# Attention loop of a perceiver block: key transposes and value products moved into the projections, with fewer value and probability buffers

## The chip, the core and the metric

The kernel runs on one core of a Trainium2 chip, as one program with five engines: TensorE (PE, with its weight loads listed as PEld), VectorE (DVE), ScalarE (ACT), GpSimd (POOL) and SyncE (SP, which issues the DMAs). The metric is the device time in microseconds. The kernel before was timed three times; its median is 3072.03 us (3068.97 to 3072.42).

## The reference

A perceiver block on 256 query tokens of width 512: a cross attention over a context of 25088 rows, a linear self attention, and an expert feed-forward part. Only the cross attention is touched. It has 16 heads of width 32 and a sigmoid in place of a softmax, so that nothing has to be normalised over the context:

```python
qh = (q @ Wq.T).reshape(B, Lq, H, D).transpose(0, 2, 1, 3)
kh = (k @ Wk.T).reshape(B, Lk, H, D).transpose(0, 2, 1, 3)
vh = (v @ Wv.T).reshape(B, Lk, H, D).transpose(0, 2, 1, 3)
qh = _layernorm(qh, gq, bq) * scale
kh = _layernorm(kh, gk, bk)
attn = jax.nn.sigmoid(jnp.einsum('bhqd,bhkd->bhqk', qh, kh))
x = jnp.einsum('bhqk,bhkd->bhqd', attn, vh)
```

## The kernel before

The context is cut into 196 tiles of 128 rows. One step of a loop handles one tile, four steps are written out per turn of the loop, and the steps are pipelined by hand: in step r TensorE projects tile r, turns and scores the keys of tile r-1, and adds up the values of tile r-2. Each engine has an instruction list of its own in a fixed order; semaphores that count upwards connect them. A wait for "tile r" is a wait for a count worked out by `n_of`.

The TensorE work of a step, in the words used below:

- P, `projection` (L1029): 24 matmuls of 512 columns with 128x128 weights. The first 12 make the centred keys in `kv_ps[:, 0]`, the last 12 make the values in `kv_ps[:, 1]`. Each operand is split in a high and a low part, hence three products for each of four pieces.
- T, `turn_keys` (L1050): four 128x128 transposes of the normalised keys `k_n` into `kv_ps[:, 1]`, the place of the values. So it waits until the values were copied away (`v_copied`), and the next value projection waits until the turned keys were split (`kt_lo_made`).
- S0 and S1, `scores` (L1063): for each half of the heads 24 matmuls with weights of 32 rows and 128 columns, four of them side by side in the array, so six groups of four. Each half fills the same four banks `s_ps`, so S1 of a tile waits for the sigmoid of S0 of that tile.
- A, `attend` (L1075): the products of probabilities and values, with weights of 128 rows and 32 columns, again four side by side. The profile lists 32 matmuls for both halves, eight groups of four.

The order of TensorE in a step is T(r-1), P(r) 1 to 24, S0(r-1), A(r-2) both halves, S1(r-1).

The others: ACT runs in a step the sigmoid of S1(r-2) (L496, 128x2048 elements), the square and a copy of the new keys (L502, L505), and the sigmoid of S0(r-1). DVE splits the turned keys (L676, L678), makes the high part of the next context tile (L669), sums the squares (L687), copies the values (L683) and scales the keys (L694). POOL makes the low part of the next context tile (L407), and for the keys an addition (L413) and a power of -0.5 (L417); the latter two stand behind the former in its list. SP loads context tiles three ahead.

There are four buffers `v_sb` for the values and three `probs` for the probabilities: S0's alternate between two, S1's always use the third.

Of the kernel before, what the change touches and what calls it, by code (L numbers as in the profile page):

```python
# [12 lines left out]
TOK, C, H, D = 256, 512, 16, 32  # L13
NK = 25088
P = 128
TT, CT = TOK // P, C // P
KT = NK // P
HG = P // D
# [77 lines left out]
def perceiver_block(nc, a, out, NKT=KT):  # L96
    f32, f32r = mybir.dt.float32, mybir.dt.float32r
    ALU, ACT, AX = mybir.AluOpType, mybir.ActivationFunctionType, mybir.AxisListType.X
    nq = (NKT - 4) // UNROLL
    life = ExitStack()  # L100
    with life:
        def sb(name, shape, dt=f32, scope=life):
            return scope.enter_context(nc.sbuf_tensor(name, shape, dt))
# [56 lines left out]
        attn = ExitStack()  # L160
# [14 lines left out]

        kt_hi = sb("kt_hi", [P, NG, P], f32r, attn)
        kt_lo = sb("kt_lo", [P, NG, P], f32r, attn)
        v_sb = [sb(f"v_sb{i}", [P, C], f32, attn) for i in range(4)]
        probs = [sb(f"probs{i}", [P, HG, 2, TOK], f32, attn) for i in range(3)]
        zeros = probs[-1][:, 0].rearrange("p j t -> p (j t)")  # L180
        psum_a = ExitStack()
        o_ps = ps("o_ps", [P, NG, TOK], psum_a)
        kv_ps = ps("kv_ps", [P, 2, C], psum_a)
        s_ps = ps("s_ps", [P, HG, 2, TOK], psum_a)
# [68 lines left out]
        s_made, probs_made, av_made = sem("s_made"), sem("probs_made"), sem("av_made")  # L253
        v_copied = sem("v_copied")
# [14 lines left out]
        def wait(eng, s, v):  # L269

            if not isinstance(v, int) or v > 0:
                eng.wait_ge(s, v)

        def n_of(it, r, per=1, more=0):

            if isinstance(it, int):
                return per * (4 * it + r) + more
            return it * (4 * per) + (per * r + more)

        def probs_of(r, half):  # L280

            return probs[2] if half else probs[r % 2]

        def is_first(it, r, t):

# [203 lines left out]
        def _(act):  # L489
            s = nc.scalar  # L490

            def sigmoid(it, r, half):

                act.wait_ge(s_made, n_of(it, r, 2, half + 1))
                wait(act, av_made, n_of(it, r, 2, 2 if half else -1))
                s.activation(probs_of(r, half)[:], s_ps[:], ACT.Sigmoid).then_inc(probs_made, 1)  # L496

            def square(it, r):

# [114 lines left out]
        def _(dve):  # L614
            v = nc.vector
# [55 lines left out]
            def split_turned(it, r):  # L671

                dve.wait_ge(t_made, n_of(it, r, 1, 1))
                wait(dve, s_made, n_of(it, r, 2))
                turned = kv_ps[:, 1].rearrange("p (g k) -> p g k", g=NG)
                v.tensor_copy(kt_hi[:], turned).then_inc(kt_hi_made, 1)  # L676
                dve.wait_ge(kt_hi_made, n_of(it, r, 1, 1))
                v.tensor_tensor(kt_lo[:], turned, kt_hi[:].bitcast(f32), ALU.subtract).then_inc(kt_lo_made, 1)  # L678

            def copy_values(it, r):  # L680
                dve.wait_ge(v_made, n_of(it, r, 1, 1))
                wait(dve, av_made, n_of(it, r, 2, -4))
                v.tensor_copy(v_sb[r % 4][:], kv_ps[:, 1]).then_inc(v_copied, 1)  # L683

            def sum_squares(it, r):
                dve.wait_ge(k_sq_made, n_of(it, r, 1, 1))
# [9 lines left out]

            def step(it, r, keys=True, more=True):

                split_turned(it, r - 1)
                if more:  # L700
                    high_part(it, r + 1)
                if keys:
                    sum_squares(it, r)
                    copy_values(it, r)
                    normalise(it, r)


# [12 lines left out]
            for c in range(CT):  # L720
# [25 lines left out]
            link(v.tensor_copy(q_hi[:], q_turned_in))  # L746
            v.tensor_tensor(q_lo[:], q_turned_in, q_hi[:].bitcast(f32), ALU.subtract)\
                .then_inc(once("q_parts_made"), 1)
            copy_values(0, 0)
            normalise(0, 0)  # L750


# [245 lines left out]
        def _(pe):  # L998
            t = nc.tensor
# [12 lines left out]
            for c in range(CT):  # L1012
                for b in range(CT):
                    dst = s_ps[:, c, b // 2, (b % 2) * P:(b % 2 + 1) * P]
                    ins = t.matmul(dst, wk[:, b, c * P:(c + 1) * P], centre[:], start=True, stop=True)
# [4 lines left out]
            for i in range(TT):  # L1020
                for c in range(CT):
                    ins = t.matmul(kv_ps[:, i], x_t[:, c, i * P:(i + 1) * P], wq[:, c],
                                   start=(c == 0), stop=(c == CT - 1))
# [10 lines left out]
            def projection(it, r, first, last):  # L1034

                for m in range(first, last):
                    if m == 0:
                        pe.wait_ge(ctx_lo_made, n_of(it, r, 1, 1))
                        wait(pe, k_kept, n_of(it, r))
                    if m == 12:  # L1040
                        wait(pe, v_copied, n_of(it, r))
                        wait(pe, kt_lo_made, n_of(it, r))
                    project(it, r, m // 12, m % 12 // 3, m % 3)

            def turn_keys(it, r):

                pe.wait_ge(k_normed, n_of(it, r, 1, 1))
                pe.wait_ge(v_copied, n_of(it, r, 1, 1))
                for grp in range(NG):
                    ins = t.transpose(kv_ps[:, 1, grp * P:(grp + 1) * P],  # L1050
                                      k_n[:, HG * grp:HG * grp + HG].rearrange("p h d -> p (h d)"), ident[:])
                ins.then_inc(t_made, 1)

            def scores(it, r, half):

                pe.wait_ge(kt_lo_made, n_of(it, r, 1, 1))
                wait(pe, probs_made, n_of(it, r, 2, half))
                for j in range(2):
                    grp = 2 * half + j
                    for n, (k, q) in enumerate(((kt_hi, q_hi), (kt_hi, q_lo), (kt_lo, q_hi))):  # L1060
                        for h in range(HG):
                            own = slice(D * h, D * h + D)
                            ins = t.matmul(s_ps[:, h, j], k[own, grp], q[own, grp],  # L1063
                                           start=(n == 0), stop=(n == 2))
                ins.then_inc(s_made, 1)

            def attend(it, r, half):

                pe.wait_ge(probs_made, n_of(it, r, 2, half + 1))
                pe.wait_ge(v_copied, n_of(it, r, 1, 1))  # L1070
                for j in range(2):
                    grp = 2 * half + j
                    for h in range(HG):
                        first = P * grp + D * h
                        ins = t.matmul(o_ps[D * h:D * h + D, grp], v_sb[r % 4][:, first:first + D],  # L1075
                                       probs_of(r, half)[:, h, j], start=False, stop=False, skip_group_check=True)
                ins.then_inc(av_made, 1)

            def step(it, r, project_it=True):

                turn_keys(it, r - 1)
                if project_it:
                    projection(it, r, 0, 24)
                scores(it, r - 1, 0)
                if not too_early(it, r - 2):
                    attend(it, r - 2, 0)
                    attend(it, r - 2, 1)
                scores(it, r - 1, 1)

            def too_early(it, r):  # L1090
# [6 lines left out]
            for i in range(2):  # L1097
                ins = t.matmul(o_ps[:, 2 * i:2 * i + 2].rearrange("p g t -> p (g t)"), zeros[:, 0:P],
                               zeros, start=True, stop=True)
# [6 lines left out]
            for grp in range(NG):  # L1106
                for i in range(TT):
                    ins = t.transpose(q_turned_in[:, grp, i * P:(i + 1) * P],
                                      big[1][:, i, grp * P:(grp + 1) * P], ident[:])
# [16 lines left out]
            for i in range(TT):  # L1126
                for c in range(CT):
                    ins = t.matmul(pm[:, i], o_t[:, c, i * P:(i + 1) * P], wp[:, c],
                                   start=(c == 0), stop=(c == CT - 1))
# [4 lines left out]
            for i in range(TT):  # L1134
                pe.wait_ge(once("x1_t_made"), i + 1)
                wait(pe, once("qkv_copied"), i)
                for k in range(3):
                    for c in range(CT):
                        ins = t.matmul(pm[:, k], mid_t[:, c, i * P:(i + 1) * P],  # L1139
                                       qkv_w[:, c, k * C:(k + 1) * C], start=(c == 0), stop=(c == CT - 1))  # L1140
                ins.then_inc(once("qkv_made"), 1)
            pe.sem_inc(w_used, 2)
            for i in range(TT):
                pe.wait_ge(once("qk_made"), i + 1)
                for k in range(2):
                    for grp in range(NG):
                        ins = t.transpose(po[:, 2 * i + k, grp * P:(grp + 1) * P],
                                          qk_max[:, i, k * C + grp * P:k * C + (grp + 1) * P], ident[:])
# [36 lines left out]
            for i in range(TT):  # L1185
                for c in range(CT):
                    ins = t.matmul(pm[:, 2 + i], mid_t[:, c, i * P:(i + 1) * P], out_w[:, c],  # L1187
                                   start=(c == 0), stop=(c == CT - 1))
# [5 lines left out]
            for i in range(TT):  # L1194
                for c in range(CT):
                    ins = t.matmul(m_ps[:, 0, i * E:(i + 1) * E], nx_t[:, c, i * P:(i + 1) * P],
                                   router_w[:, c], start=(c == 0), stop=(c == CT - 1))
            ins.then_inc(once("logits"), 1)
            pe.wait_ge(once("gates"), 1)
            for i in range(TT):  # L1200
                ins = t.transpose(m_ps[0:E, 1, i * P:(i + 1) * P], rt[:, 5, i], ident[:])
            ins.then_inc(once("gates_turned"), 1)
            pe.wait_ge(once("gate_split"), 1)
            for e in range(E):

                for part in range(2):
                    ins = t.matmul(f_ps[:, e // 2, (e % 2) * TOK:(e % 2 + 1) * TOK],
                                   pick[:, e:e + 1].to_broadcast([E, P]), gate_parts[:, part],
                                   start=(part == 0), stop=(part == 1))
# [137 lines left out]
```

## Time and profile before

| | |
|---|---|
| median of three runs | 3072.03 us |
| the profiled execution | 3068.97 us |
| its span, first to last instruction | 3067.2 us |
| the attention loop | from about 75 us to about 1985 us of the span |
| TensorE busy | 2923.6 us, 95% |
| VectorE, ScalarE, GpSimd busy | 49%, 46%, 37% |

Times of rows are microseconds from the start of the span. A timeline row has a start, a duration, engine, line, operation, written tile, read tiles, and a count of instructions merged; square brackets tell how long the engine had been idle and which engine released it. The matmuls overlap, so the distance between two starts tells their pace, and the duration is a latency. For four matmuls side by side one row stands for the group.

### The profile page before, as it was taken

Reading aid. Unit: us, or ns where it says so; the run is one execution under the profiler, and the core shown is the slowest. Engines: PE = TensorE matmul, PEld = TensorE weight load, DVE = VectorE, ACT = ScalarE, POOL = GpSimd, SP = SyncE. Lnnn points to the kernel's source line nnn. Section 1 sums busy time; section 2 is a strip of 40 time slices with the busy share of each in tenths; the row PEclk is TensorE's granted clock in tenths of the full one; section 3 lists DMA queues with packets and bytes.
Section 4 is the critical chain, followed back from the end, with each engine's and each line's share of the span. In section 5 each row is a group of like instructions: output and inputs, shape, how many; then the busy total and the mean of one; then the engine's idle time right before and its main releaser. Section 6 shows DMA issues by size and latency. Waiting matters only on the chain.

```text
span 3067.2 us, 71038 instructions
## 1 busy us (share of the span) xinstructions
PE 2923.6 (95%) x28530; PEld 2355.4 (77%) x28530; DVE 1505.4 (49%) x2020; ACT 1417.4 (46%) x1277; POOL 1137.0 (37%) x856
## 2 busy tenths in 40 slices
PE   6999999999999999999999999976999999999998
PEld 4777777777777777777777777745998988999987
DVE  5333333333333333333333333346477766578877
ACT  1444444445444444444444444422445445455444
POOL 3444444444444444444444444401031423032322
PEclk8999999999999999999999999987999999999999
DMA  5000000000000000000000001001545445555443
GB/s 199 28 24 27 27 27 24 27 27 24 27 27 26 26 27 27 24 27 27 24 27 27 27 24 27 11 28 69 192 166 184 173 165 192 192 179 179 157 162 141
DMA packets 53229, 231.78 MB, mean 76 GB/s; under 512 B 6040, under 2 KB 6296, under 8 KB 31776
## 3 DMA queue, kind: packets, MB, share of 16 engines
q1 hardware_dynamic: 53152, 230.73, 22.1%
q8 instruction: 50, 0.82, 0.1%
q14 instruction: 27, 0.22, 0.0%
HBM read 230.19 MB, written 0.52 MB: 75 GB/s over the span
## 4 chain that ended last, share of the span: by engine, by line
PE 75%; ACT 13%; DVE 6%; issue 4%; DMA 1%; POOL 1%; ACTq 0%; DVEq 0%; SPq 0%; POOLq 0%
PE kv_ps L1029 34%; PE f_ps L1270 18%; PE s_ps L1063 12%; ACT probs L496 12%; PE kv_ps L1050 4%; PE y_ps L1257 4%; DVE stage L884 1%; DMA w_raw<-w_dram 1%; ACT w_hi L535 1%; DVE w_lo L628 1%; PE pm L1139 1%; DVE h_hi L883 1%; DVE sums L921 1%; POOL h_lo L470 0%; PE pm L1187 0%
## 5 line engine op out<-in xcount | busy, mean ns | idle before, releaser
L496 ACT ACTIVATE probs<-s_ps 128x2048 f32<-128x2048 f32 x392 | 737.0, 1880 | 713.6 <-PE s_ps L1063 713.6
L407 POOL TENSOR_TENSOR ctx_lo<-ctx_raw,ctx_hi 128x512 fp32r<-128x512 f32 x196 | 252.0, 1286 | 905.3 <-DVE ctx_hi L669 905.3
L417 POOL TENSOR_TENSOR k_var<-k_var,neg_half 128x16 f32<-128x16 f32 x196 | 570.7, 2912 | 15.5 <-POOL k_var L413 0.2
L470 POOL TENSOR_TENSOR h_lo<-stage,h_hi 128x256 f32 x240 | 255.3, 1078 | 695.8 <-DVE h_hi L886 388.1
L628 DVE TENSOR_TENSOR w_lo<-w_raw,w_hi 128x2048 fp32r<-128x2048 f32 x164 | 383.1, 2340 | 168.4 <-ACT w_hi L535 167.6
L1270 PE MATMUL f_ps<-h_hi,w_hi 128*128 128x256 f32 x1536 | 428.0, 279 | 14.8 <-POOL h_lo L470 14.8
L1270 PE MATMUL f_ps<-h_lo,w_hi 128*128 128x256 f32 x1536 | 426.8, 278 | 0.0
L1270 PE MATMUL f_ps<-h_hi,w_lo 128*128 128x256 f32 x1536 | 426.6, 278 | 0.0
L1075 PE MATMUL o_ps<-probs,v_sb 128*32 128x256 f32 x6272 | 380.9, 383 | 1.0 <-ACT probs L496 1.0
L535 ACT ACTIVATE w_hi<-w_raw 128x2048 fp32r<-128x2048 f32 x164 | 313.1, 1912 | 138.7 <-DMA w_raw<-w_dram 100.9
L1029 PE MATMUL kv_ps<-wk_hi,ctx_hi 128*128 128x512 f32 x784 | 324.1, 413 | 1.5 <-issue 1.5
L676 DVE CAST kt_hi<-kv_ps 128x512 fp32r<-128x512 f32 x196 | 135.5, 691 | 373.5 <-PE kv_ps L1050 373.5
L1029 PE MATMUL kv_ps<-wk_lo,ctx_hi 128*128 128x512 f32 x784 | 307.9, 393 | 0.0
L1029 PE MATMUL kv_ps<-wk_hi,ctx_lo 128*128 128x512 f32 x784 | 307.7, 392 | 0.0
L1029 PE MATMUL kv_ps<-wv_hi,ctx_hi 128*128 128x512 f32 x784 | 305.1, 389 | 0.0
L1029 PE MATMUL kv_ps<-wv_hi,ctx_lo 128*128 128x512 f32 x784 | 305.0, 389 | 0.0
L1029 PE MATMUL kv_ps<-wv_lo,ctx_hi 128*128 128x512 f32 x784 | 304.8, 389 | 0.0
L1270 PEld LDWEIGHTS f_ps<-h_hi,w_hi 128*128 128x128 f32 x1536 | 291.1, 190 | 15.7 <-POOL h_lo L470 15.6
L1063 PEld LDWEIGHTS s_ps<-q_hi,kt_hi 32*128 32x128 f32 x3136 | 153.7, 183 | 192.4 <-ACT probs L496 117.6
L1063 PE MATMUL s_ps<-q_hi,kt_hi 32*128 32x256 f32 x3136 | 269.6, 329 | 29.2 <-ACT probs L496 11.5
L1270 PEld LDWEIGHTS f_ps<-h_hi,w_lo 128*128 128x128 f32 x1536 | 291.2, 190 | 0.0
L1270 PEld LDWEIGHTS f_ps<-h_lo,w_hi 128*128 128x128 f32 x1536 | 291.1, 190 | 0.1
(191 smaller groups left out, 4896.7 us busy)
## 6 DMA issues: line engine op xcount, KB each, us to landing
w_raw<-w_dram SPq DMA_DIRECT2D x160, 1024.0 KB, 4.8
ctx_raw<-ctx_dram SPq DMA_DIRECT2D x196, 256.0 KB, 2.6
qkv_w<-qkv_w_dram SPq DMA_DIRECT2D x1, 3072.0 KB, 13.2
bias_rows<-bias_rows_dram SPq DMA_DIRECT2D x1, 1280.0 KB, 16.6
wq<-wq_dram SPq DMA_DIRECT2D x1, 1024.0 KB, 5.6
wk_rows<-wk_dram SPq DMA_DIRECT2D x1, 1024.0 KB, 7.6
wv<-wv_dram SPq DMA_DIRECT2D x1, 1024.0 KB, 9.7
out_w<-out_w_dram SPq DMA_DIRECT2D x1, 1024.0 KB, 17.7
```

The costliest lines, as they stand in the source:

```text
L407: g.tensor_tensor(ctx_lo[r % 2][:], raw[r % 4][:], ctx_hi[r % 2][:].bitcast(f32), ALU.subtract).then_inc(ctx_lo_made, 1)
L417: g.tensor_tensor(k_var[:, 2], k_var[:, 1], neg_half[:].to_broadcast([P, H]), ALU.pow)\
L470: g.tensor_tensor(lo, stage[i][:], hi.bitcast(f32), ALU.subtract)\
L496: s.activation(probs_of(r, half)[:], s_ps[:], ACT.Sigmoid).then_inc(probs_made, 1)
L535: s.activation(w_hi[i][:], w_raw[i % RAW][:], ACT.Copy).then_inc(w_hi_made, 1)
L628: v.tensor_tensor(w_lo[i][:], w_raw[i % RAW][:], w_hi[i][:].bitcast(f32), ALU.subtract)\
L676: v.tensor_copy(kt_hi[:], turned).then_inc(kt_hi_made, 1)
L1029: ins = t.matmul(kv_ps[:, which], left[r % 2][:, c], right[:, c], start=(c == 0 and n == 0), stop=(c == CT - 1 and n == 2))
L1050: ins = t.transpose(kv_ps[:, 1, grp * P:(grp + 1) * P], k_n[:, HG * grp:HG * grp + HG].rearrange("p h d -> p (h d)"), ident[:])
L1063: ins = t.matmul(s_ps[:, h, j], k[own, grp], q[own, grp], start=(n == 0), stop=(n == 2))
L1075: ins = t.matmul(o_ps[D * h:D * h + D, grp], v_sb[r % 4][:, first:first + D], probs_of(r, half)[:, h, j], start=False, stop=False, skip_gr ...
L1270: ins = t.matmul(f_ps[:, slot, 0:TOK], w[:, k, cols], r[:, k], start=(k == 0 and m == 0), stop=(k == kt - 1 and m == 2))
```

## The change

TensorE's order in a step becomes P(r) 1 to 6, T(r-1), P(r) 7 to 12, A(r-2) both halves, S0(r-1), P(r) 13 to 24, S1(r-1). So the key half of the projection is cut in two by the transposes, the value products come before S0, and the value half of the projection stands between S0 and S1.

The buffers become two `v_sb` and two `probs`, one for each half of the heads. With them the waits change: the sigmoid of a half now waits for the value products of the same half of the tile before, and the copy of the values of tile r waits for the value products of tile r-2. The DVE copy of the values of tile r moves from step r, between the sum of squares and the scaling of the keys, to the head of step r+1, right behind the scaling of the keys of tile r.

```diff
-        v_sb = [sb(f"v_sb{i}", [P, C], f32, attn) for i in range(4)]
-        probs = [sb(f"probs{i}", [P, HG, 2, TOK], f32, attn) for i in range(3)]
+        v_sb = [sb(f"v_sb{i}", [P, C], f32, attn) for i in range(2)]
+        probs = [sb(f"probs{i}", [P, HG, 2, TOK], f32, attn) for i in range(2)]
...
             def sigmoid(it, r, half):
 
                 act.wait_ge(s_made, n_of(it, r, 2, half + 1))
-                wait(act, av_made, n_of(it, r, 2, 2 if half else -1))
-                s.activation(probs_of(r, half)[:], s_ps[:], ACT.Sigmoid).then_inc(probs_made, 1)
+                act.wait_ge(av_made, n_of(it, r, 2, half + 1))
+                s.activation(probs[half][:], s_ps[:], ACT.Sigmoid).then_inc(probs_made, 1)
...
             def copy_values(it, r):
                 dve.wait_ge(v_made, n_of(it, r, 1, 1))
-                wait(dve, av_made, n_of(it, r, 2, -4))
-                v.tensor_copy(v_sb[r % 4][:], kv_ps[:, 1]).then_inc(v_copied, 1)
+                wait(dve, av_made, n_of(it, r, 2))
+                v.tensor_copy(v_sb[r % 2][:], kv_ps[:, 1]).then_inc(v_copied, 1)
...
             def step(it, r, keys=True, more=True):
 
+                copy_values(it, r - 1)
                 split_turned(it, r - 1)
                 if more:
                     high_part(it, r + 1)
                 if keys:
                     sum_squares(it, r)
-                    copy_values(it, r)
                     normalise(it, r)
...
             def step(it, r, project_it=True):
 
+                if project_it:
+                    projection(it, r, 0, 6)
                 turn_keys(it, r - 1)
                 if project_it:
-                    projection(it, r, 0, 24)
-                scores(it, r - 1, 0)
+                    projection(it, r, 6, 12)
                 if not too_early(it, r - 2):
                     attend(it, r - 2, 0)
                     attend(it, r - 2, 1)
+                scores(it, r - 1, 0)
+                if project_it:
+                    projection(it, r, 12, 24)
                 scores(it, r - 1, 1)
```

`probs_of` goes, `attend` reads `v_sb[r % 2]` and `probs[half]`, and the single `copy_values(0, 0)` ahead of the loop is now in the first step.

## Rows read from the trace of the kernel before

**Rows 1.** Busy time by engine in 200 us of the loop (clock: PEclk).
```profile
500.00:700.00 200.00, 197.37 (x2192) 147.00 (x2188) 75.84 (x121) 97.24 (x81) 89.03 (x61) 1.00 0.09 26
```

**Rows 2.** Waits between 1000 and 1980 us: total, times, longest.
```profile
PEld s_ps L1063 <- ACT probs L496: 60.6, 99, 0.7
```

**Rows 3.** The chain that ended last, 1009.9 to 1020.1 us: start, duration.
```profile
1008.17 1.89 ACT probs L496
...
1010.10 0.98 PE s_ps L1063 x22
1011.08 0.59 PE kv_ps L1050 x4
...
1017.14 0.94 PE s_ps L1063 x24
```

**Rows 4.** Timeline of TensorE, from S0 of one step to S0 of the next.
```profile
1007.84 0.29 PE L1063 MATMUL s_ps<-q_hi,kt_lo 32*128 32x256 f32 x4
...
1009.59 0.40 PE L1075 MATMUL o_ps<-probs,v_sb 128*32 128x256 f32 x4
1010.10 0.39 PE L1063 MATMUL s_ps<-q_hi,kt_hi 32*128 32x256 f32 x4
1010.32 0.29 PE L1063 MATMUL s_ps<-q_lo,kt_hi 32*128 32x256 f32 x4
...
1010.79 0.29 PE L1063 MATMUL s_ps<-q_hi,kt_lo 32*128 32x256 f32 x4
1011.01 0.66 PE L1050 MATMUL kv_ps<-ident,k_n 128*128 128x128 f32 x4
1011.42 0.48 PE L1029 MATMUL kv_ps<-wk_hi,ctx_hi 128*128 128x512 f32 x1
1011.74 0.39 PE L1029 MATMUL kv_ps<-wk_hi,ctx_lo 128*128 128x512 f32 x1
...
1016.75 0.39 PE L1029 MATMUL kv_ps<-wv_lo,ctx_hi 128*128 128x512 f32 x1
1017.07 0.39 PE L1063 MATMUL s_ps<-q_hi,kt_hi 32*128 32x256 f32 x4
```

**Rows 5.** Same timeline, first value-product group of that step (merged with the second).
```profile
1008.06 0.64 PE L1075 MATMUL o_ps<-probs,v_sb 128*32 128x256 f32 x8
```

**Rows 6.** The transposes, 1000 to 1980 us: duration ns minimum, median, maximum.
```profile
L1050 PE MATMUL kv_ps<-ident,k_n x396: 272/273/330, 1001.1 to 1976.5; 128*128 128x128 f32 x198
```

**Rows 7.** Timeline of TensorE behind the loop, linear attention.
```profile
2063.50 0.28 PE L1170 MATMUL po<-masked,ones 128*32 128x128 f32 x4
...
2063.72 0.73 PE L1156 MATMUL pm<-qk_t 32*128 32x256 f32 x8
```

**Rows 8.** Timeline of TensorE, first projection of the kernel, after a pause.
```profile
28.67 0.47 PE L1029 MATMUL kv_ps<-wk_hi,ctx_hi 128*128 128x512 f32 x1 [1.48 <-issue]
28.98 0.39 PE L1029 MATMUL kv_ps<-wk_hi,ctx_lo 128*128 128x512 f32 x1
```

**Rows 9.** Timeline of ScalarE: S0's sigmoid in three steps in a row.
```profile
102.71 1.88 ACT L496 ACTIVATE probs<-s_ps 128x2048 f32<-128x2048 f32 x1 [2.55 <-PE s_ps L1063]
...
112.72 1.88 ACT L496 ACTIVATE probs<-s_ps 128x2048 f32<-128x2048 f32 x1 [2.55 <-PE s_ps L1063]
...
122.65 1.88 ACT L496 ACTIVATE probs<-s_ps 128x2048 f32<-128x2048 f32 x1 [2.55 <-PE s_ps L1063]
```

**Rows 10.** Timeline of the other engines in one step, 1011 to 1020 us.
```profile
1012.52 0.69 DVE L678 TENSOR_TENSOR kt_lo<-kv_ps,kt_hi 128x512 fp32r<-128x512 f32 x1
...
1013.62 1.28 POOL L407 TENSOR_TENSOR ctx_lo<-ctx_raw,ctx_hi 128x512 fp32r<-128x512 f32 x1 [4.50 <-DVE ctx_hi L669]
...
1014.46 0.60 ACT L502 ACTIVATE k_sq<-kv_ps 128x512 f32<-128x512 f32 x1 [1.45 <-PE kv_ps L1029]
...
1016.15 2.91 POOL L417 TENSOR_TENSOR k_var<-k_var,neg_half 128x16 f32<-128x16 f32 x1
...
1018.10 1.88 ACT L496 ACTIVATE probs<-s_ps 128x2048 f32<-128x2048 f32 x1 [2.55 <-PE s_ps L1063]
1019.14 0.68 DVE L694 TENSOR_TENSOR k_n<-k_centred,k_var 128x496 f32<-128x496 f32 x1 [1.27 <-POOL k_var L417]
```

**Rows 11.** Timeline at the loop's two ends: S1 of the first tile, keys of the last.
```profile
63.37 0.58 PE L1063 MATMUL s_ps<-q_hi,kt_hi 32*128 32x256 f32 x4 [2.07 <-ACT probs L496]
...
1994.45 2.78 DVE L694 TENSOR_TENSOR k_n<-k_centred,k_var 128x496 f32<-128x496 f32 x1 [1.40 <-POOL k_var L417]
```

More of the change, by code:

```diff
@@ L278, in n_of @@
             return it * (4 * per) + (per * r + more)
-        def probs_of(r, half):
-            return probs[2] if half else probs[r % 2]
         def is_first(it, r, t):
@@ L748, in _ @@
                 .then_inc(once("q_parts_made"), 1)
-            copy_values(0, 0)
             normalise(0, 0)
@@ L1074, in attend @@
                         first = P * grp + D * h
-                        ins = t.matmul(o_ps[D * h:D * h + D, grp], v_sb[r % 4][:, first:first + D],
-                                       probs_of(r, half)[:, h, j], start=False, stop=False, skip_group_check=True)
+                        ins = t.matmul(o_ps[D * h:D * h + D, grp], v_sb[r % 2][:, first:first + D],
+                                       probs[half][:, h, j], start=False, stop=False, skip_group_check=True)
                 ins.then_inc(av_made, 1)
             def step(it, r, project_it=True):
+                if project_it:
+                    projection(it, r, 0, 6)
                 turn_keys(it, r - 1)
                 if project_it:
-                    projection(it, r, 0, 24)
-                scores(it, r - 1, 0)
+                    projection(it, r, 6, 12)
                 if not too_early(it, r - 2):
```

## The prediction

> **What bounds the kernel.** I read the windows by engine first: in 200 us of the loop TensorE is busy 197.37 us at a granted clock of 1.00, its upper level of 2.4 GHz, and no other engine for even half of the time [rows 1]. That is no proof that nothing waits, because a matmul's duration is its latency and hides short gaps. The list of waits shows the one that is left: TensorE's weight loads wait for the sigmoid once in every step, 99 times in 98 steps, 60.6 us in all, about 0.61 us each [rows 2]. The chain that ended last gives the structure: S0, its sigmoid of 1.89 us, S1, the transposes, the projection, S0 again [rows 3]. The value products are not in it, they lie beside the sigmoid. A step is 9.93 us long: 6.97 from S1 to the next S0, 0.70 from S0's first group to its last, and 2.26 from there to S1 again [rows 4]. What the change can remove is the part of the sigmoid that sticks out behind the value products.
>
> How far it sticks out is read from start to start in TensorE's timeline [rows 4, 5]. First each kind's own pace: a projection matmul (1016.75 - 1011.74) / 22 = 0.228 us; a group of four score matmuls (1010.79 - 1010.32) / 4 = 0.118; a group of value products, 1.53 us from the first start to the last of eight, 0.02 less for a slow first one, gives 0.216. Then the distance from the last start of one kind to the first of the next, less the own pace of the former:
>
> - S0 to A: 1008.06 - 1007.84 - 0.12 = 0.10
> - A to S1: 1010.10 - 1009.59 - 0.22 = 0.29
> - S1 to T: 1011.01 - 1010.79 - 0.12 = 0.10
> - P to S0: 1017.07 - 1016.75 - 0.23 = 0.09
>
> Three switches cost 0.10 each with no wait in them; A to S1 costs 0.29. What it would be without the sigmoid is seen once behind the loop, in the same two shapes: column-wise products last start at 2063.50, scores at 2063.72, own pace 0.107 (128 columns against the 256 of a 0.216), so 0.11 again [rows 7]. The stall that can be removed is 0.29 - 0.10 = 0.19 us, not the 0.61 of the waits: these count from the end of the last weight load, and the matmuls go on behind it.
>
> A second price follows each switch: the first matmul of a kind holds up the second, since its weights are not there yet. For S the second group starts 0.22 after the first in place of 0.12: 0.10 [rows 4]. For T the first takes 0.330 against 0.273: 0.06 [rows 6]. For P after a pause 28.98 - 28.67 - 0.23 = 0.08 [rows 8]. From T to P nothing of either kind is paid: from the first transpose to the second projection matmul are 0.73 us [rows 4], and four transposes at 0.11, one projection at 0.228 and the 0.06 of the first transpose make that.
>
> **The change, part by part, per step.**
>
> 1. *The stall goes.* P 13 to 24 now lies between S0 and S1, 12 x 0.228 = 2.7 us against a sigmoid of 1.88 that starts 0.33 behind S0's last group (1018.10, one step after 1007.84 + 9.93) [rows 4, 10]. Minus 0.19.
> 2. *A moves ahead of S0.* P to A takes the place of S0 to A, A to S0 that of A to S1, each at 0.10 plus the same first load: zero beyond item 1. P to A is in no row; from both sides 0 and 0.19 (the dearest switch with no wait, P to S with S's first load); I take 0.10, like the four that I can read.
> 3. *A step now ends S1 to P, not S1 to T.* The 0.10 stays, the first load is P's 0.08 in place of T's 0.06: plus 0.02.
> 4. *S0 to P 13 is new*: 0.10 + 0.08 = plus 0.18. A switch from S to P is in no row. Below: nothing, as from T to P. Above: 0.20, as S pays. I take 0.18, since S to T, which leaves the same shape for the same full array, pays its 0.10 in every step.
> 5. *P to T is new* and in no row. Both use the full array, like T to P, which is free: 0. Above: 0.16, as S to T. The second T to P is the old one.
> 6. *The turn of the loop.* Every fourth step is longer, 10.01 in place of 9.93 [rows 9], and the lateness sits on ACT: the same sigmoid comes late. Off the path that costs nothing: minus 0.08 / 4 = minus 0.02. If TensorE's own branch shows instead, this is zero.
>
> The Trainium skill, TensorEngine Tiling (Array Packing), section Tiling Modes, Key Properties, says that changing the tiling mode, not just the tile, drains TensorE. By that rule S to P pays the drain and T to P, P to T pay none, which is the sum as it stands; without the rule the two S to P could be taken at 0.10 less each, 39 us over the loop. The trace agrees on the four switches and the one non-switch that it has. Read as a count the rule speaks against the change: five changes of mode in a step where there were four.
>
> Sum: -0.19 + 0.02 + 0.18 - 0.02 = -0.01 us in a step. Laid out from its first P at 0, the new step reads T 1.45, P7 1.80, A 3.36, S0 5.21, P13 6.12, S1 9.03, next P 9.94; against a mean of 9.95 before. Over 194 steps: minus 2 us.
>
> **Do the waits hold at that pace?** All must be done when TensorE comes. The sigmoid of S1 runs to 1.99, A's second half needs it at about 4.2. The turned keys' low part ends 2.20 behind T's start (1012.52 + 0.69 - 1011.01), at 3.65; S0 needs it at 5.21. S0's sigmoid ends at 8.1, S1 comes at 9.03. The longest is the key chain. The square starts at 3.46 (0.44 behind P12's start); its sum is ready at 4.8, but POOL first makes the context's low part, which waits for DVE, and runs from 4.2 to 5.5; then 0.3 for the addition and 2.91 for the power: 8.7. The scaling of the keys ends at 9.5, and behind it in DVE's list the copy of the values (0.69) at 10.2. T needs both at 11.4: 1.2 us to spare [rows 10]. Queued behind that copy is the split of the turned keys, which waits for T anyway. With two buffers each, the value copy waits for products finished 3 us earlier and the sigmoids for products that stand ahead of their scores: nothing. SP's loads are three tiles ahead: nothing.
>
> **The ends.** In the first step S1 waited 2.07 us for S0's sigmoid [rows 11]; P 13 to 24 now covers it, though a table load of ScalarE keeps about 1 of it, and P 1 to 6 start beside the first scaling of the keys: about -2 to -3. At the last tile the scaling took 2.78 us in place of 0.68 beside a POOL operation [rows 11]; now the value copy is queued behind it, and S1 has no P behind S0: about +1. Together -2.
>
> **Total.** -2 -2 = -4 us: the profiled execution's 3068.97 becomes 3065; the median lies 3.06 above the profiled one, so the median becomes 3068.
>
> **Rivals.**
>
> *The new switch is free (faster).* If leaving S for P costs nothing at either place, a step is 0.36 shorter, 70 us: 2998. If only the first load is hidden, 0.16 a step: 3037. For it: weight loads of P are hidden behind T. Against: every row that leaves S pays. Chance 0.17, mostly the milder form.
>
> *P to T pays (slower).* Cutting the projection costs 0.16 as S to T does, or P's first load is dearer: up to 0.16 x 194 = 31 us, 3099. For it: no row shows this direction. Against: T to P is free. It ends slower from 0.03 us a step on. Chance 0.18.
>
> *The value copy becomes the wait (slower).* It decides when the key chain is 1.2 us later than laid out. The row for it is the scaling at 2.78 us beside a POOL operation: +2.1 in each step would make T wait 0.9, 175 us, 3243. Against: in the loop POOL is idle when the scaling runs, since it waits for POOL's power. Chance 0.05, and 0.05 for something that I don't see.
>
> **Numbers.** My forecast, a step between 0.05 shorter and 0.05 longer, has 0.55: 3058 to 3080, most likely 3068. A measurement of this kernel tells 0.2%, 6 us, from no change: same is 3066 to 3078. A third of the forecast's weight lies below that, a tenth above it. Faster: 0.17 + 0.19 = 0.36. Slower: 0.05 + 0.16 of P to T's + 0.05 = 0.26. Same: 0.38. The range for 8 in 10 reaches into the milder forms on both sides: 3040 to 3096.
>
> **What will show it.** Right: no wait of TensorE for the sigmoid, S0 to P and S1 to P at 0.21 between starts with 0.31 to the second matmul, P to T at 0.23, A to S0 at 0.32, a step of 9.94, the value copy ending 1.2 us ahead of T. Wrong: P to T above 0.3; S to P at 0.12; T released by `v_sb` or `k_n`; a granted clock below 1.00 in the loop.

## The result, and the profile after

The changed kernel takes 3095.18 us (median, 3084.19 to 3101.03), the one before 3072.03 (3064.05 to 3076.56), seven runs of each. The ratio is 1.0075 with a 95% interval of 1.0055 to 1.0094: 23 us slower, clear of noise, where the forecast was 4 us faster. The time lies just inside the stated range of 3040 to 3096, at its upper end.

The windows by engine, the same 200 us of the loop as in [rows 1]:

```profile
500.00:700.00 200.00, 200.00 (x2140) 143.89 (x2136) 74.49 (x119) 96.04 (x79) 86.11 (x60) 1.00 0.10 26
```

TensorE has gone from 197.37 to 200.00 us busy, and fewer matmuls start in the window (2140 in place of 2192), so fewer steps fit. The work of a step is the same; the busy share rose and the time rose with it. The stall was removed, and the time went into distances between starts that count as busy.

The list of waits between 1000 and 1980 us, where [rows 2] had the sigmoid:

```profile
DVE k_n L690 <- POOL k_var L413: 354.2, 97, 3.7
...
PEld s_ps L1058 <- issue: 74.1, 194, 0.4
PEld o_ps L1070 <- issue: 35.6, 98, 0.4
```

No other engine releases TensorE any more. What is left, "issue", is time in which the engine waited for nothing that the profile shows. The chain that ended last, in order of time, shows the same for one step; where [rows 3] had a sigmoid, it is TensorE alone:

```profile
1008.70 1.59 PE kv_ps L1024 x6
1010.28 0.44 PE kv_ps L1045 x4
1010.72 1.39 PE kv_ps L1024 x6
1012.12 1.86 PE o_ps L1070 x32
1013.98 0.91 PE s_ps L1058 x24
1014.89 2.97 PE kv_ps L1024 x12
```

TensorE's timeline of that step, against [rows 4, 5]:

```profile
1008.41 0.29 PE L1058 MATMUL s_ps<-q_hi,kt_lo 32*128 32x256 f32 x4
1008.63 0.50 PE L1024 MATMUL kv_ps<-wk_hi,ctx_hi 128*128 128x512 f32 x1
1008.96 0.40 PE L1024 MATMUL kv_ps<-wk_hi,ctx_lo 128*128 128x512 f32 x1
...
1009.89 0.39 PE L1024 MATMUL kv_ps<-wk_lo,ctx_hi 128*128 128x512 f32 x1
1010.12 0.60 PE L1045 MATMUL kv_ps<-ident,k_n 128*128 128x128 f32 x4
1010.48 0.48 PE L1024 MATMUL kv_ps<-wk_hi,ctx_hi 128*128 128x512 f32 x1
...
1011.72 0.40 PE L1024 MATMUL kv_ps<-wk_lo,ctx_hi 128*128 128x512 f32 x1
1012.04 1.93 PE L1070 MATMUL o_ps<-probs,v_sb 128*32 128x256 f32 x32
1013.91 0.40 PE L1058 MATMUL s_ps<-q_hi,kt_hi 32*128 32x256 f32 x4
...
1014.60 0.29 PE L1058 MATMUL s_ps<-q_hi,kt_lo 32*128 32x256 f32 x4
1014.82 0.50 PE L1024 MATMUL kv_ps<-wv_hi,ctx_hi 128*128 128x512 f32 x1
1015.15 0.40 PE L1024 MATMUL kv_ps<-wv_hi,ctx_lo 128*128 128x512 f32 x1
1015.39 0.40 PE L1024 MATMUL kv_ps<-wv_lo,ctx_hi 128*128 128x512 f32 x1
...
1017.47 0.39 PE L1024 MATMUL kv_ps<-wv_lo,ctx_hi 128*128 128x512 f32 x1
1017.79 0.39 PE L1058 MATMUL s_ps<-q_hi,kt_hi 32*128 32x256 f32 x4
```

Every step of the changed loop is 10.073 us long (the transposes start at 73.30 and, 192 steps later, at 2007.38); before it was 9.950 (75.75 and 1986.17). Times 192 that is 23.7 us. Up to the first of these starts 2.5 us were saved, behind the last of them to the last value product 0.7; the part behind the attention, whose instructions are the same, took 5.8 longer in this pair of executions. Together 26.3, the difference of the two profiled executions (3095.31 and 3068.97). Over the eleven profiles of this study the part behind the last value product takes 1058.6 to 1060.6 us in the five kernels that keep the value half of the projection ahead of both halves of the scores, and 1058.3 to 1069.9 in the six with the changed order. So the 5.8 can't be put down to chance or to the change from what is here; the loss in the loop, 23.7 us, is there without it.

Where the 0.123 us of a step come from, in medians over the loop, from start to start. Here and below a distance that begins at scores or value products is taken from the last single matmul, which starts 0.02 behind its group's row (the prediction counted from the row). The projection's steady pace, reached late in an uninterrupted run, is 0.227; "excess" is what a run takes beyond it. "Switch" is the distance beyond the own pace of the kind that is left.

| part of a step | before | after | difference |
|---|---|---|---|
| A to the scores | 0.492 | 0.309 | -0.183 |
| the turn of the loop, per step | 0.021 | 0 | -0.021 |
| S0 to P 13, new: switch 0.098, excess of the run 0.154 | | 0.252 | +0.252 |
| P 1 to 6 behind S1: excess | | 0.130 | +0.130 |
| T, first start to last | 0.383 | 0.327 | -0.056 |
| P behind T: excess | 0.116 | 0.108 | -0.008 |
| into A (from S, now from P), beyond the own pace | 0.096 | 0.100 | +0.004 |
| P 6 to T | | 0.005 | +0.005 |

The excess behind T before is read from the same timeline as [rows 4], where the intervals behind the first are 0.23, 0.24, 0.23, 0.23, 0.23 until the pace is reached:

```profile
1011.97 0.40 PE L1029 MATMUL kv_ps<-wk_lo,ctx_hi 128*128 128x512 f32 x1
...
1012.90 0.39 PE L1029 MATMUL kv_ps<-wk_hi,ctx_hi 128*128 128x512 f32 x1
```

The other engines in the step after, against [rows 10]:

```profile
1007.91 0.69 DVE L679 COPY v_sb<-kv_ps 128x512 f32<-128x512 f32 x1 [0.20 <-PE kv_ps L1024]
...
1014.14 2.91 POOL L413 TENSOR_TENSOR k_var<-k_var,neg_half 128x16 f32<-128x16 f32 x1
1014.93 1.88 ACT L492 ACTIVATE probs<-s_ps 128x2048 f32<-128x2048 f32 x1 [1.69 <-PE s_ps L1058]
1017.13 0.67 DVE L690 TENSOR_TENSOR k_n<-k_centred,k_var 128x496 f32<-128x496 f32 x1 [3.67 <-POOL k_var L413]
```

The value copy ends at 1008.60, 1.5 us ahead of the transposes at 1010.12; S0's sigmoid ends at 1016.81, 1 us ahead of S1. No wait took the place of the one removed.

### The profile page after: what moved, and what is told of

It is laid out like the page before. It is cut to its first block, busy times and chain, and to the rows that moved or that the text cites. A ratio compares the mean times of both kernels' runs of the same rounds, so it can differ in the third digit from the quotient of the medians.

```text
span 3093.6 us, 71184 instructions
## 1 busy us (share of the span) xinstructions
PE 2977.9 (96%) x28530; PEld 2344.2 (76%) x28530; DVE 1504.8 (49%) x2020; ACT 1418.1 (46%) x1277; POOL 1131.1 (37%) x856
## 4 chain that ended last, share of the span: by engine, by line
PE 89%; DVE 5%; issue 2%; ACT 1%; DMA 1%; POOL 1%; ACTq 0%; DVEq 0%; SPq 0%; POOLq 0%
PE kv_ps L1024 37%; PE f_ps L1269 19%; PE o_ps L1070 12%; PE s_ps L1058 12%; PE y_ps L1256 4%; PE kv_ps L1045 3%; DVE stage L879 1%; PE pm L1138 1%; ACT w_hi L531 1%; DMA w_raw<-w_dram 1%; DVE h_hi L878 1%; DVE w_lo L624 0%; DVE sums L916 0%; POOL h_lo L466 0%; PE pm L1186 0%
## 5 line engine op out<-in xcount | busy, mean ns | idle before, releaser
L690 DVE TENSOR_TENSOR k_n<-k_centred,k_var 128x496 f32<-128x496 f32 x196 | 134.4, 686 | 711.6 <-POOL k_var L413 711.6
L1024 PE MATMUL kv_ps<-wk_hi,ctx_hi 128*128 128x512 f32 x784 | 347.5, 443 | 4.3 <-DVE q_lo L743 2.8
L1024 PE MATMUL kv_ps<-wv_hi,ctx_hi 128*128 128x512 f32 x784 | 330.0, 421 | 0.0
L1070 PEld LDWEIGHTS o_ps<-probs,v_sb 128*32 128x32 f32 x6272 | 184.2, 110 | 174.0 <-issue 72.9
L1024 PE MATMUL kv_ps<-wk_lo,ctx_hi 128*128 128x512 f32 x784 | 310.3, 396 | 0.0
L1024 PE MATMUL kv_ps<-wv_lo,ctx_hi 128*128 128x512 f32 x784 | 308.3, 393 | 0.0
L1024 PE MATMUL kv_ps<-wk_hi,ctx_lo 128*128 128x512 f32 x784 | 307.4, 392 | 0.0
L1024 PE MATMUL kv_ps<-wv_hi,ctx_lo 128*128 128x512 f32 x784 | 306.0, 390 | 0.0
L1269 PEld LDWEIGHTS f_ps<-h_hi,w_hi 128*128 128x128 f32 x1536 | 290.7, 189 | 14.0 <-POOL h_lo L466 13.9
```

The lines of the kernel that those rows point to most:

```text
L690: v.tensor_tensor(k_n[:, :, 0:D - 1], k_c[:, :, 0:D - 1], per_row(k_var[:, 2], D - 1), ALU.mult)\
L1024: ins = t.matmul(kv_ps[:, which], left[r % 2][:, c], right[:, c], start=(c == 0 and n == 0), stop=(c == CT - 1 and n == 2))
L1070: ins = t.matmul(o_ps[D * h:D * h + D, grp], v_sb[r % 2][:, first:first + D], probs[half][:, h, j], start=False, stop=False, skip_group_ch ...
L1269: ins = t.matmul(f_ps[:, slot, 0:TOK], w[:, k, cols], r[:, k], start=(k == 0 and m == 0), stop=(k == kt - 1 and m == 2))
```

## The experiments

Nine kernels. "Step" is the mean distance between transposes in the steady loop, read from each trace. A ratio is to the kernel before on the same chip, with its 95% interval. e2, e7 and e9 were executed once each, so they have a step but no ratio.

**e1, the order alone.** The changed order with the old number of buffers:

```diff
-        v_sb = [... for i in range(2)]
-        probs = [... for i in range(2)]
+        v_sb = [... for i in range(4)]
+        probs = [... for i in range(3)]
...
-                act.wait_ge(av_made, n_of(it, r, 2, half + 1))
+                wait(act, av_made, n_of(it, r, 2, 2 if half else -1))
...
-                wait(dve, av_made, n_of(it, r, 2))
+                wait(dve, av_made, n_of(it, r, 2, -1))
```

> The changed order with the old buffers: four value buffers, three probability buffers. Theory (the 26 us come from TensorE's own stream, nothing waits for a buffer): the step stays at 10.07 us and the time at 1.0075 of before, within 0.1%. Rival (two buffers each make something wait): the time falls back by a part of 23 us.

Measured: step 10.073, each distance the same to 0.001 us, ratio 1.0082 (1.0054 to 1.0110). The number of buffers and the sigmoid's wait have no part in the loss. The value copy's wait was not set free here: it is one count short of the changed kernel's, the first half of tile r-2's products in place of both. But in the changed kernel's list of waits the copy stands only behind the projection (`DVE v_sb L679 <- PE kv_ps L1024`, 13.9 us in 73 waits), never behind value products.

**e2, a sigmoid that leaves PSUM alone.** I had noticed that the slow intervals of the projection fall beside the sigmoid.

```diff
-                s.activation(probs[half][:], s_ps[:], ACT.Sigmoid)
+                s.activation(probs[half][:].rearrange("p h j t -> p (h j t)"), w_raw[1][:], ACT.Sigmoid)
```

> The changed kernel, but the sigmoid reads a weight tile in SBUF of the same size and not the scores in PSUM; it waits for the scores as before. The probabilities are therefore not those of the scores. Theory (projection matmuls are slower while ScalarE reads PSUM: 0.233 us against 0.227, and 0.335 against 0.310 from the first to the second): with the read gone the pace is 0.227 throughout, the 12 value matmuls run 2.58 us from first to last start in place of 2.65, the step is 9.95 to 9.99. Rival 1 (the slower pace belongs to the first microseconds after a change of tiling): 2.65 and 10.07 stay. Rival 2 (it is the sigmoid's write to SBUF, or its activity at all): they stay as well, and the two rivals then have to be told apart by a shorter sigmoid.

```profile
1007.83 0.50 PE L1025 MATMUL kv_ps<-wk_hi,ctx_hi 128*128 128x512 f32 x1
1007.95 1.92 ACT L492 ACTIVATE probs<-w_raw 128x2048 f32<-128x2048 f32 x1 [1.97 <-PE s_ps L1059]
1008.17 0.40 PE L1025 MATMUL kv_ps<-wk_hi,ctx_lo 128*128 128x512 f32 x1
1008.40 0.40 PE L1025 MATMUL kv_ps<-wk_lo,ctx_hi 128*128 128x512 f32 x1
```

In this timeline the sigmoid reads `w_raw`, and the projection starts as in the changed kernel: 0.34, then 0.23. Value matmuls 2.65 us, step 10.073, nothing moved; its one execution took 3091.23 us. The theory fell: that the sigmoid reads PSUM beside the projection costs nothing here. That it is not the sigmoid's activity at all is seen in the changed kernel's very first projection, in the timeline ahead of the loop, with ScalarE idle until 31.14, when the slow intervals are over:

```profile
28.09 0.47 PE L1024 MATMUL kv_ps<-wk_hi,ctx_hi 128*128 128x512 f32 x1 [1.48 <-issue]
28.40 0.40 PE L1024 MATMUL kv_ps<-wk_hi,ctx_lo 128*128 128x512 f32 x1
28.63 0.40 PE L1024 MATMUL kv_ps<-wk_lo,ctx_hi 128*128 128x512 f32 x1
...
31.14 0.60 ACT L498 ACTIVATE k_sq<-kv_ps 128x512 f32<-128x512 f32 x1 [29.04 <-PE kv_ps L1024]
```

Its 24 matmuls take 5.339 us from first to last start, with the full slow row (0.306, 0.235, 0.233, 0.236, 0.224, 0.231, 0.236, 0.228, 0.233, 0.231, then 0.227). The same run in the kernel before, which starts with [rows 8], takes 5.297 without it:

```profile
29.21 0.39 PE L1029 MATMUL kv_ps<-wk_lo,ctx_hi 128*128 128x512 f32 x1
...
33.97 0.39 PE L1029 MATMUL kv_ps<-wv_lo,ctx_hi 128*128 128x512 f32 x1
```

**e3, the stall alone.** The kernel before with three of the sigmoid's four banks:

```diff
-                s.activation(probs_of(r, half)[:], s_ps[:], ACT.Sigmoid).then_inc(probs_made, 1)
+                s.activation(probs_of(r, half)[:, 0:3], s_ps[:, 0:3], ACT.Sigmoid).then_inc(probs_made, 1)
```

> The kernel before, with a sigmoid over three of the four banks (1536 of 2048 columns, about 1.45 us); the fourth part of the probabilities is a constant. So the stall behind the value products is gone and no switch is added. Theory (stall 0.19 us in a step plus 0.02 for ScalarE's loop turn): value products to S1 falls from 0.49 to 0.30 to 0.31 us between starts, the step from 9.95 to 9.74, the time by 40 us, ratio 0.987. Rival (the stall was larger than what start to start shows, 0.6 as the waits list it): the step falls by more, up to 120 us.

TensorE's timeline of e3, from value products to S1, and the sigmoid beside it:

```profile
1005.88 1.93 PE L1077 MATMUL o_ps<-probs,v_sb 128*32 128x256 f32 x32
1007.74 0.39 PE L1065 MATMUL s_ps<-q_hi,kt_hi 32*128 32x256 f32 x4
```
```profile
1006.07 1.45 ACT L498 ACTIVATE probs<-s_ps 128x1536 f32<-128x1536 f32 x1 [2.55 <-PE s_ps L1065]
```

The sigmoid ends at 1007.52 and S1 starts at 1007.74, 1.86 us behind the value products, as in the changed kernel (1012.04 to 1013.91). A to S1 is 0.309, the step 9.747, shorter by 0.203, the ratio 0.9877 (0.9848 to 0.9905). So the stall was worth what start to start says, 0.18 and the loop turn's 0.02, and not the 0.6 that the list of waits shows. The same list for e3, 1000 to 1980 us, still has an entry for the sigmoid, 0.4 us each time, though nothing is left of the stall between starts:

```profile
PEld s_ps L1065 <- ACT probs L498: 39.5, 96, 0.4
```

The projection's run, 5.330 us, did not change with the shorter sigmoid either.

**e4, the transposes inside the projection, all else as before.**

```diff
             def step(it, r, project_it=True):
 
-                turn_keys(it, r - 1)
                 if project_it:
-                    projection(it, r, 0, 24)
+                    projection(it, r, 0, 3)
+                turn_keys(it, r - 1)
+                if project_it:
+                    projection(it, r, 3, 24)
```

> The kernel before, with the four transposes behind the third projection matmul, all else as before. Theory (leaving the scores for a projection costs 0.10 for the switch and 0.11 for the first load while the sigmoid runs, where the transposes paid 0.10 and 0.06; projection to transposes is free): the step grows by 0.05 to 0.07 us, 10 to 14 us, ratio 1.003 to 1.005. Rival (P to T costs a switch too): 0.15 or more a step, 30 us. Rival (no price for either): no change.

Step 10.018, longer by 0.068; ratio 1.0049 (1.0030 to 1.0068). S1 to P is 0.205, the second matmul 0.337 behind the first, P to T 0.232 at a pace of 0.227. The rival that P to T costs a switch is out, and so is the one that neither costs anything; leaving the scores for the projection is dearer than leaving them for the transposes.

**e5, one switch more in the changed kernel.**

```diff
                 if not too_early(it, r - 2):
                     attend(it, r - 2, 0)
-                    attend(it, r - 2, 1)
                 scores(it, r - 1, 0)
+                if not too_early(it, r - 2):
+                    attend(it, r - 2, 1)
```

> The changed kernel with the value products cut in two around S0: A's first half, S0, A's second half, P 13 to 24. One change of tiling more in a step, nothing else. Theory (a change costs 0.10 between starts, and value products 0.03 for their first load): the step grows by 0.12 us, from 10.07 to 10.19, the ratio to before is 1.015. On the slow start of the projection there are two readings, both open: if TensorE's feed is exhausted by the dense scores, P 13 to 24 now follows the sparser value products and runs at 0.227 from its second matmul on, so the step is 10.15; if every restart of the projection is slow, the intervals 0.235, 0.233, 0.236 stay. Rival (switches cost nothing, the 0.12 us of the change come from somewhere else): 10.07 stays.

```profile
1013.34 0.29 PE L1058 MATMUL s_ps<-q_hi,kt_lo 32*128 32x256 f32 x4
1013.55 1.07 PE L1070 MATMUL o_ps<-probs,v_sb 128*32 128x256 f32 x16
1014.56 0.50 PE L1024 MATMUL kv_ps<-wv_hi,ctx_hi 128*128 128x512 f32 x1
1014.89 0.40 PE L1024 MATMUL kv_ps<-wv_hi,ctx_lo 128*128 128x512 f32 x1
...
1015.82 0.39 PE L1024 MATMUL kv_ps<-wv_lo,ctx_hi 128*128 128x512 f32 x1
...
1017.18 0.39 PE L1024 MATMUL kv_ps<-wv_lo,ctx_hi 128*128 128x512 f32 x1
```

Step 10.187, longer than the changed kernel's by 0.114, where 0.12 was expected; ratio 1.0120 (1.0096 to 1.0144), below the expected 1.015, though the step fits. Switches cost, with no other work and no wait added. Behind the value products the projection still pays 0.34 for its first distance, but its row of slow intervals is shorter, five in place of ten, the first counted in (mean 0.337, 0.236, 0.228, 0.232, 0.231, then 0.227; the last six take (1017.18 - 1015.82) / 6 = 0.227), which saves 0.02 of the 0.14 that the switch costs. That lies between the two readings.

**e6, one restart of the projection less.** The changed kernel with the transposes straight behind S1:

```diff
-                if project_it:
-                    projection(it, r, 0, 6)
                 turn_keys(it, r - 1)
                 if project_it:
-                    projection(it, r, 6, 12)
+                    projection(it, r, 0, 12)
```

> The changed kernel without the cut of the key projection: transposes straight behind S1, then P 1 to 12. One restart of the projection less (two in place of three). Theory, summed from measured distances (S to T 0.204, T 0.383, T to P 0.028, P 12 matmuls 2.61, the rest as in the changed kernel): step 10.00 in place of 10.07, ratio to before 1.005. Rival (the transposes were cut in to give the value copy time, and now wait for it): S to T above 0.4 between starts, step above 10.2, T released by the value copy or the scaling of the keys.

Scores and transposes in TensorE's timeline, and the value copy in the other engines':

```profile
1009.92 0.29 PE L1058 MATMUL s_ps<-q_hi,kt_lo 32*128 32x256 f32 x4
1010.25 0.52 PE L1045 MATMUL kv_ps<-ident,k_n 128*128 128x128 f32 x3
```
```profile
1009.42 0.69 DVE L679 COPY v_sb<-kv_ps 128x512 f32<-128x512 f32 x1 [0.46 <-PE kv_ps L1024]
```

Step 10.067, ratio 1.0078 (1.0051 to 1.0105), where 10.00 and 1.005 were expected: as good as the changed kernel. S to T is 0.323 in place of 0.204. T needs the place of the values, and it starts 0.145 to 0.147 us behind the end of the value copy in every step (here 1010.11), which points to the copy as what it waits for; the list of waits names none. While T is held up its own slow start shrinks, its run takes 0.355 in place of 0.383. Without the hold-up the step would be 10.067 - 0.12 + 0.03 = 9.98, an estimate from these rows, 0.02 below the 10.00 summed, as the slow rows came out shorter. Both theories hold in part: by that estimate the restart costs about 0.1, and the cut hides a wait of about that size. Cutting the transposes in gained nothing, and lost nothing.

**e7 and e8, the stall covered by the transposes.** An attempt to keep the gain without a second restart, in the kernel before:

```diff
-                turn_keys(it, r - 1)
                 if project_it:
                     projection(it, r, 0, 24)
                 scores(it, r - 1, 0)
                 if not too_early(it, r - 2):
                     attend(it, r - 2, 0)
                     attend(it, r - 2, 1)
+                if project_it:
+                    turn_keys(it, r)
                 scores(it, r - 1, 1)
```

e8 adds to it, so that the keys are ready earlier:

```diff
-                g.tensor_tensor(k_var[:, 1], k_var[:, 0], k_eps[:].to_broadcast([P, H]), ALU.add)\
-                    .then_inc(k_var_made, 1)
-                pool.wait_ge(k_var_made, n_of(it, r, 1, 1))
...
-                s.activation(k_sq[:].rearrange("p h d -> p (h d)"), kv_ps[:, 0], ACT.Square,
+                s.activation(k_sq[:, :, 0:D], kv_ps[:, 0].rearrange("p (h d) -> p h d", h=H), ACT.Square,
```

> The kernel before with the transposes of the new tile between the value products and S1, to cover the rest of the sigmoid with work that has to be done anyway. Out of the measured distances: P 24 after scores 5.37, P to S 0.318, S 0.71, S to A 0.203, A 1.555, A to T 0.293, T 0.383, T to S 0.206, S 0.706, S to P 0.203: 9.95, against 9.95 before, plus a wait for the scaling of the keys of up to 0.1 us. So no gain, 9.95 to 10.05. Rival (covering a stall with needed work gains the stall): 9.76.

> The kernel of e7 with one GpSimd operation less in the key chain: the 1e-5 is a 33rd summand of the sum of squares, so that the addition of 0.21 us goes and the scaled keys are ready 0.29 us earlier. Theory: the wait of T for the keys is gone, step 9.95, ratio to before 0.999 to 1.001. Rival (the chain was no wait): same as e7 within 0.02 us in a step.

The waits of e7, 1000 to 1980 us:

```profile
PEld kv_ps L1050 <- DVE k_n L694: 44.8, 99, 0.5
```

e7: step 9.978, no gain, as expected; its one execution took 3075.18 us. The sigmoid is gone from TensorE's waits, and the keys are in it: A to T 0.333, in place of 0.310 without a wait. In e8 it is 0.310 in every step (its list still has 40.7 us for the keys, as e3's had for the sigmoid), and the step is 9.980: what was won came back in the projection's run behind S1, 5.350 us in e7 and 5.388 in e8. Ratio of e8 1.0021 (1.0008 to 1.0034), against the 0.999 to 1.001 and the step of 9.95 expected; the rival's figure came true, though not for its reason, since the wait was there in e7. So a stall of 0.18 was covered with work that has to be done, and nothing was gained: five switches in place of four, and the projection begun behind scores.

**e9, fewer score matmuls.** A test of why the projection starts slowly, on the changed kernel:

```diff
-                    for n, (k, q) in enumerate(((kt_hi, q_hi), (kt_hi, q_lo), (kt_lo, q_hi))):
+                    for n, (k, q) in enumerate(((kt_hi, q_hi), (kt_hi, q_lo))):
```

> The changed kernel, but the scores leave out the third of their three products (low part of the keys): 16 matmuls in place of 24 in each S, four groups in place of six. The scores are therefore a little less precise. The distances at the switches should not depend on it: 0.20, 0.31, 0.32. The step falls by 2 x 2 x 0.118 = 0.47 us, to 9.60. Open is the slow start of the projection, ten intervals of 0.224 to 0.236 behind S. Reading 1 (TensorE's feed falls behind in the dense scores and catches up in the projection): with a third less of them the row of slow intervals behind S1 is shorter, four to seven, and the step is 9.57 or less. Reading 2 (every restart has it, whatever stood before): ten slow intervals stay.

```profile
1000.84 0.29 PE L1058 MATMUL s_ps<-q_lo,kt_hi 32*128 32x256 f32 x4
...
1001.06 0.50 PE L1024 MATMUL kv_ps<-wv_hi,ctx_hi 128*128 128x512 f32 x1
1001.40 0.40 PE L1024 MATMUL kv_ps<-wv_hi,ctx_lo 128*128 128x512 f32 x1
1001.64 0.40 PE L1024 MATMUL kv_ps<-wv_lo,ctx_hi 128*128 128x512 f32 x1
...
1003.72 0.39 PE L1024 MATMUL kv_ps<-wv_lo,ctx_hi 128*128 128x512 f32 x1
```

Step 9.62, where 9.60 was summed and reading 1 wanted 9.57 or less; its one execution took 3011.35 us, against 3069.74. Twelve value matmuls take 1003.72 - 1001.06 = 2.66 us from first to last start, as long as behind 24 score matmuls, with all eleven intervals slow. Reading 1, with four to seven such intervals, fell for this place. Behind S1 all five intervals are slow too, but they are those of e5's short row (0.337, 0.236, 0.228, 0.233, 0.231) and the transposes cut the run there, so its length is not seen.

## Why the prediction was wrong

The structure held, and the sign did not. The stall went (forecast 0.19, in the trace 0.18; e3 by itself 0.20 with the loop turn), the loop turn of ScalarE no longer showed (0.02 forecast, 0.021), no wait took its place, the margins were as laid out or better (value copy 1.5 us against 1.2), P to T was free (0.005), the buffers were neutral, and the ends gave 3.1 us where 2 were forecast. The switch from scores to the projection has its 0.10 between starts at both places. The rule of the Trainium skill quoted in the prediction (TensorEngine Tiling (Array Packing), section Tiling Modes, Key Properties) says that a change of tiling mode drains TensorE; the trace agrees, and e5 adds the price of one more, 0.114 a step net.

What failed are two terms of the sum that were too small, items 4 and 3, both of them the price of starting the projection behind scores. The parts of the sum nearly cancelled, so they turned its sign:

- *Item 4, S0 to P 13, "I take 0.18".* It costs 0.252. The first load was taken from [rows 8], after a pause, as 0.08; behind scores the second start comes 0.335 after the first, so 0.108. And the run does not then go at its pace: nine intervals between 0.224 and 0.236 follow, 0.046 beyond the pace in all. The stated upper bound of 0.20 did not hold it.
- *Item 3, "plus 0.02".* It costs 0.066: 0.130 of excess in P 1 to 6, less 0.056 of the transposes' own slow start and 0.008 behind them.
- Item 2 and the rest of the A row are 0.01 off, item 5 0.005.

Together 0.133 us in a step, 194 times: 26 us, which with the forecast of -4 makes 22, about the measured 23. The pace of 0.228 was an average over the 22 intervals behind the first, (1016.75 - 1011.74) / 22, of which the longer ones stand at the start; spread evenly, they cannot be seen to belong to the start. The change makes three starts of one.

The rival with the right sign, "P to T pays", came near with its 3099, but by luck: its 0.16 stood at the wrong place, P to T costs 0.005. Its half sentence "or P's first load is dearer" is what came true, at 2 x 0.03, which is half of the 0.12 that items 3 and 4 are off; the slow intervals are the other half. The rival "the new switch is free" is refuted by e5 and by the S to P distances. The wait for the value copy is real once the transposes are not cut in (e6), but not in the changed kernel.

What stays open is what sets the slow row. It is not the sigmoid (e2, e3, and the first projection with ScalarE idle), and a third fewer score matmuls ahead did not shorten it between S0 and P 13 (e9). It is shorter behind transposes (five intervals beyond the first, in e3 as well, where TensorE is held up by nothing), in e6 and e7, where TensorE had waited, and behind value products (e5); it is full in e8 and behind S0 in e9, where nothing waits. It does not hang on TensorE's own instructions alone: the first projection of a kernel stands behind the same TensorE instructions in all of them, and its run takes 5.297 us in the kernel before and in e8, 5.339 in the changed one and in e3, and 5.296 to 5.334 in the others. No run showed the cause, so the part of the loss that lies in these rows may come out otherwise in another kernel.

## What to carry to other kernels

A stall on the busiest engine is worth only its distance from start to start beyond the unstalled distance, and filling it with other work costs one more border between kinds of matmul: here 0.20 us of stall and loop turn against 0.25 for the border and 0.07 for the step's other start of the projection behind scores. Price each new border between kinds of matmul from the same border in the trace, read interval by interval and not from an average pace, and where two such sums nearly cancel give the range more weight than the sign. Once the busiest engine never waits, the borders in a step are what is left to count, and their kinds with them: e8 and the changed kernel both have five, and their steps are 9.980 and 10.073, with one start of the projection behind scores against two.

## What the runs showed of the hardware

After each interruption the 512-column matmuls do not go at their pace at once. In the loop the first interval takes 0.31 to 0.34 us, then 4 to 10 more between 0.224 and 0.240 follow before they settle at 0.227, at a granted clock of 1.00. The slow intervals are mostly the tail of one sequence (0.341, 0.240, 0.235, 0.233, 0.236, 0.224, 0.231, 0.236, 0.228, 0.233, 0.231, the whole of it in e8). Only the first projection of the kernel before and of two others goes without them. None of this was expected.

Whether the sigmoid beside the projection reads PSUM or SBUF makes no difference (e2).

Each change between the three shapes (scores, value products, full array) costs 0.09 to 0.11 us between starts beyond the own pace, whichever kind follows. Between projection and transposes, which use the same full array, there is none (0.232 at a pace of 0.227).

A wait that the list charges to a weight load can stand there though no matmul starts later for it: 0.4 us each time in e3, where the value products and the next scores are 0.309 apart, as in the changed kernel, where no engine is waited for.
